# Attention loops of a two-layer model: the rows of scores are placed behind the products with the values

## The reference

```
xn = layernorm(x, g_in)
q = (xn @ Wq).reshape(b, n, 16, 64).transpose(0, 2, 1, 3) * scale
k, v = split(xn @ Wkv)                 # one head for all, after the null key and value
sim = einsum('bhid,bjd->bhij', q, k) + bias
sim = where(causal_mask, neg, sim); sim = where(mask_p, sim, neg)
attn = softmax(sim, axis=-1)
out = einsum('bhij,bjd->bhid', attn, v)
return layernorm(out.reshape(b, n, 1024) @ Wo, g_out)
```

## Time and profile before

| | us |
|---|---|
| median of 3 runs | 3386.32 (3378.21 to 3391.15) |
| the profiled execution | 3392.3 |
| its span, first to last instruction | 3390.5 |
| TensorE busy | 3055.6 (90%) |
| VectorE busy | 1947.1 (57%) |
| ScalarE busy | 1551.8 (46%) |
| GpSimd busy | 289.9 (9%) |

### The profile page before, as it was taken

The page is one execution under the profiler, slowest core; times in us unless marked ns, Lnnn a source line. Parts: engine busy times, 40 slices in busy tenths (PEclk is TensorE's granted clock), DMA queues, the critical chain, the costliest instruction groups (busy, mean ns, idle before and its releaser), DMA issues. The chain is left out here.

```text
span 3390.5 us, 50330 instructions
## 1 busy us (share of the span) xinstructions
PE 3055.6 (90%) x17338; PEld 2117.3 (62%) x17338; DVE 1947.1 (57%) x4655; ACT 1551.8 (46%) x3708; POOL 289.9 (9%) x605
## 2 busy tenths in 40 slices
PE   7999799989999999855879999997999999959996
PEld 5555566654677777533457777775477777736764
DVE  3556455535676765785757777535477677442223
ACT  1110355542666664454446666524266666313332
POOL 0003000000011110000000000000011111002222
PEclk8998899989999999886989999998999999979998
DMA  1007433127344441010542222102734444341112
GB/s 39 19 14 161 52 47 47 14 74 222 114 140 130 145 134 46 1 29 2 156 121 80 70 82 69 41 2 74 222 117 148 120 144 136 117 145 34 33 34 90
DMA packets 233450, 293.70 MB, mean 87 GB/s; under 512 B 25502, under 2 KB 178334, under 8 KB 233073
## 3 DMA queue, kind: packets, MB, share of 16 engines
q1 hardware_dynamic: 229466, 280.39, 29.8%
q0 software_dynamic: 3744, 10.23, 1.0%
HBM read 222.01 MB, written 68.10 MB: 86 GB/s over the span
## 5 line engine op out<-in xcount | busy, mean ns | idle before, releaser
L2076 ACT ACTIVATE cond_p<-cond_p,cond_negm 128x128 f32<-128x128 f32 (+7 forms) x768 | 593.1, 775 | 419.9 <-DVE cond_negm L2107 419.2
L2057 PE MATMUL ps_o<-cond_pt,cond_v 128*64 128x256 f32 (+1 forms) x3840 | 480.5, 371 | 5.2 <-DVE attn_out L2143 0.5
L2035 PE MATMUL ps_s<-cond_k_high,cond_q_high 128*128 128x512 f32 (+3 forms) x1152 | 443.5, 391 | 15.9 <-DVE cond_negm L2107 7.7
L2107 DVE CUSTOM_DVE_ANT_0 cond_p<-ps_s,cond_side,cond_null_scores 128x128 f32<-128x128 f32 (+7 forms) x512 | 404.0, 811 | 32.2 <-PE ps_s L2037 26.1
L2037 PE MATMUL ps_s<-cond_k_both,cond_q_both 128*128 128x512 f32 (+3 forms) x1152 | 390.4, 351 | 0.0
L2047 PE MATMUL ps_t<-ident,cond_p 128*128 128x128 f32 x2304 | 350.5, 282 | 6.7 <-ACT cond_pt L2081 4.8
L2057 PEld LDWEIGHTS ps_o<-cond_pt,cond_v 128*64 128x64 f32 x3840 | 237.9, 136 | 168.5 <-issue 70.7
L2047 PEld LDWEIGHTS ps_t<-ident,cond_p 128*128 128x128 f32 x2304 | 251.0, 141 | 107.2 <-issue 78.4
L1179 ACT ACTIVATE attn_pt<-ps_t 128x512 f32<-128x512 f32 (+3 forms) x384 | 172.7, 490 | 251.3 <-PE ps_t L1140 196.8
L2035 PEld LDWEIGHTS ps_s<-cond_k_high,cond_q_high 128*128 128x128 f32 x1152 | 222.7, 193 | 49.3 <-DVE cond_negm L2107 20.1
L2115 DVE COPY cond_pt<-ps_t 128x512 f32<-128x512 f32 (+1 forms) x240 | 140.3, 585 | 167.3 <-PE ps_t L2047 165.5
(11 more groups left out here) (430 smaller groups left out, 4782.9 us busy)
## 6 DMA issues: line engine op xcount, KB each, us to landing
mqa_q_halves<-cond_q_cut SPq DMA_DIRECT2D x96, 512.0 KB, 5.8
cond_q_both<-mqa_q_halves SPq DMA_DIRECT2D x384, 128.0 KB, 3.3
cond_q_high<-mqa_q_halves SPq DMA_DIRECT2D x192, 128.0 KB, 2.9
cond_side<-in_fside_16xSxS SPq DMA_DIRECT2D x32, 512.0 KB, 7.3
moe_experts<-in_L_ffn_W SPq DMA_DIRECT2D x16, 1024.0 KB, 12.3
cond_side<-in_fside_16xSxS SPq DMA_DIRECT2D x32, 448.0 KB, 5.8
cond_side<-in_fside_16xSxS SPq DMA_DIRECT2D x32, 384.0 KB, 5.1
cond_side<-in_fside_16xSxS SPq DMA_DIRECT2D x32, 320.0 KB, 4.6
```

The costliest lines, as they stand in the source:

```text
L2035: nc.tensor.matmul(m.S[k % 2][:, lo:hi], c32(a.Q1[i][:, h, s * P:(s + 1) * P]), c32(a.K1[:, keys]), start=True, stop=False)
L2057: last = nc.tensor.matmul(sums[u % ON][h * HD:(h + 1) * HD, s0 * P:2 * P], a.V[:, b * QB + kb, :], PT[c % PT_SLOTS][:, (2 * h + s0) * P:(h ...
L2076: nc.scalar.activation(p, p, ACT.Exp, bias=negm[u % SMALL][:, r:r + 1], scale=-1.0, accum_out=rsum[u % SMALL][:, r:r + 1]).then_inc(exped, 1)
L2107: nc.vector.tensor_tensor_reduce(out=probs(u, r, 0, q + 1), in0=m.S[k % 2][:, 0:L], in1=toep_back(u, h, L) if cosine else a.side[h][:, SID ...
```

## The change

The first of the two calls of `place` in each group is gone. It stood between the group's turns and its spread and attends, and placed up to two rows. The second call, behind the attends, now places all rows of the group. Nothing else differs: the same instructions, waits, buffers and transfers. (Lines from there on have a number lower by one.)

More of the change, by code:

```diff
@@ L1331, in mqa_order @@
                 finished = u
-            place(ROWS_AHEAD, 2)
             if spreads and n_groups - spreads[0][0] >= 2:
```

## The result

The changed kernel took **3506.68 us** (median of 4 runs, 3503.06 to 3515.6) against 3386.18 (4 runs, 3378.21 to 3391.15): a ratio of 1.0359, with a 95% interval of 1.0337 to 1.0382. It is slower by 120.5 us in the medians, and by 110.8 in the two profiled executions (3503.06 against 3392.3). The prediction was 3500, with 3420 to 3560 as its range.

What follows compares the result with a forecast made beforehand. TensorE was taken to bound the kernel, with VectorE and ScalarE hidden behind it. Pauses of 101 us, 8 for GpSimd waits and 6 for slow clock make 115; 3392 + 115 - 6, rounded, gives 3500 us, range 3420 to 3560.

Steps and rivals of the forecast that it cites:

- The round: One round of the loops, four units in ten groups: TensorE idles 2.2 us more, 101 us over 46 rounds.
- The chain: Sums on VectorE, exponential and turn copy on ScalarE lose attends as cover: TensorE idles 1.2 and 0.5 us a round.
- the first pause: Third group of a round: its first turn waits for ScalarE's copy, TensorE idle 1.2 us.
- the second pause: Fourth group of a round: its first turn waits for ScalarE's copy, 10.2 against 9.65, 0.5 us idle.
- The four small rows: Rows of 1, 2, 1, 2 blocks follow each other with two score buffers: TensorE idle 0.5 us a round.
- The switches of TensorE: TensorE's changes between kinds of work: cost taken as nothing; 0.1 us on some 460 groups would be 46 us.
- GpSimd and the half clock: Spreads wait 8 us more for GpSimd's copy; half clock speed behind two more long waits costs 6 us.
- The cover is enough: Rival, 15%: the chain fits its cover nearly everywhere, only the four small rows cost; 3423 us.
- The clock falls too: Rival, 8%: half speed on TensorE follows each round's pauses, adding 3 us a round, 138 in all; 3640 us.
- Faster: Rival, 5%: the chain fits its cover, biases transfer earlier, waits for GpSimd and some slow clock go; 3361 us.
- No difference: Rival, 4%: the gain and the four small rows' 23 us cancel; 3386 us.
- What would show it: Signs in the loops: TensorE busy 99.5% to some 93%, clock 1.00, turns waiting for ScalarE's copy about 90 times.

Runs made afterwards that it cites:

- E3: Changed kernel, with two of the four small rows (one and two blocks) placed ahead of the attends again: 3496.77 us, ratio 1.0326.
- e10: Changed kernel, with two of the four small rows ahead of the attends again and GpSimd's last mask one unit later: 3449.52 us, ratio 1.0197.
- e7: Kernel before the change, with GpSimd's mask of the last quarter of the biases one unit later in its queue: 3362.12 us, ratio 0.9936.
- e9: Changed kernel, with GpSimd's mask of the last quarter of the biases one unit later in its queue: 3467.18 us, ratio 1.0251.

## Why the prediction was right, and where it was not

**The round** was to grow by 2.2 us and grew by 2.24 in the second loop. The mechanism of two of its parts was right; that the sum came out so close was luck, with its parts off in both directions.

**The chain**: predicted pauses of 1.2 and 0.5 us, together 1.7 a round; measured 1.04 and 0.25 in the usual round (1.25 and 0.28 in the one that was followed), and 1.1 a round by the short exponentials. The place, the engines and the first pause were right. Two things were mis-sized. The first is the second pause. By my steps TensorE would reach that turn at 9.65 and the copy be seen at 10.2; it reached it at 10.03 (1939.93 less 1929.90) and the turn began at 10.31. TensorE was later than I had it by 0.4: 0.3 at the first pause, the rest in the switches. The chain was later by only 0.1, since ScalarE's spread copy begins 0.46 us after a turn's copy (1935.99 to 1936.45), not 0.57. A pause of TensorE is cover for the chain's next pass: pauses in one loop don't simply add. The second is the base. I wrote that between the starts of the earlier trace rows no time is lost, and 0.18 us a round was, at the attend of 1947.34, which waited for the late product. The change took this pause away, so the chain's net cost is 1.3 − 0.18 = 1.1.

**The four small rows**: predicted 0.5, measured 0.45 to 0.50 as a distance. E3's round is 0.41 shorter and e10 faster by 18 us, 0.38 in each of 46 rounds. Right.

**The switches of TensorE**, which I cost at nothing: this step failed. I took attend to row for turn to row and left out the third pair, turn to attend. Two full turns take 0.84 us ahead of a row, and 0.96 ahead of an attend (1929.90 to 1930.86); turns with a half one took 0.76 ahead of an attend and 0.63 ahead of a row. Some of it comes back where rows now stand ahead of turns: a row of seven takes 0.92 there and took 0.98 ahead of attends. What remains is 2.24 − 1.1 − 0.5 = 0.64 us a round, 30 us over 47 rounds. The bound that I named for this step, 46 us at 0.1 us a group, was of the right kind, and I should have taken something from it.

**GpSimd and the half clock**, predicted 8 + 6 = 14 us: the waits grew from 20.0 to 22.0 us, in 11 times and not 14, the clock behind them took about 3 us less and not 6 more, and e7 and e9 together give 1.4 us in the profiled executions. As a size it was too large there; the timed runs allow up to the full 14, and beyond. This stays open.

In all, over 47 rounds: chain 1.1 × 47 = 52 (predicted 78), small rows 0.5 × 47 = 24 (23), switches 0.64 × 47 = 30 (0). With 1.4 for GpSimd and the clock this makes 107, against 110.8 in the profiled executions; with the 15 that the medians give, 121 against 120.5. Two errors of some 25 to 30 us, one each way, cancelled.

**The rivals.** *The cover is enough* is refuted: turns waited 46.0 us in 55 times. *The clock falls too* is refuted: with pauses in every round the granted clock is 1.00 from 1780 to 2180. The swing that the Trainium skill, TensorE: Matmul & The Clock Gate, section "A second HAM failure mode: psum-queue depth-cycling", reports for short pauses does not show here at pauses of up to 1.25 us, twice in some 30 us. *Faster* needed a chain 1 us shorter, and the last mask shows that its 25 us are real but come from another edit (a gain of the early product there is, the 0.18 us a round at the attend). *No difference* fell with it.

**What would show it.** The busy share was to fall to 93%, and it fell to 96.2%. The time lost is as said (7% fewer instructions in the stretch), but the modelled ends cover part of it, and I had myself called distances the safer reading. For the same reason the waits are listed 55 times and not 90: the second pause of each round is in none of the lists. Durations stayed, the product waited longer for the spread's copy, and all of the extra time lies in the loops, as said.

## What to carry to other kernels

Where one engine is full and the others hide behind it, ask what lies between an instruction that starts a chain and the instruction that needs its end: the products between a row of scores and the next transposes were the time in which sums, exponential and copy ran. Moving work that no one waits for cost 3.6% here with no instruction added. Undoing one link of such a chain moved the wait in these runs (the late product to the attends, the small rows to the long row's buffer, the long rows to the seams of two orders), so judge an edit by the length of a round, not by the wait that it removes. And check on several rounds that the one you read instruction by instruction is the usual one.

## What the hardware showed beside it

- Two turns on TensorE ahead of an attend are 0.12 us longer than ahead of a row (0.96 against 0.84), with the same instructions and no wait listed. It is so with short exponentials too (0.97 in the new order, 0.85 in the old one). The trace doesn't tell why.
- Waits of TensorE cost more than their length in the first and third loops: 20.0 us of waits for GpSimd in the old order cost 29.9 us, and 22.0 in the new one 31.3. The clock behind some of them explains most of it: an estimated 8 of the 9.9 us beyond the waits in the old order, 5 of the 9.3 in the new one. It did not go by the length of the wait alone: it was 0.72 in the 6 us behind one of 1.83 us (907.13) and 1.00 behind one of 3.19 (2718.43). The rest stays open. Pauses of 1.04 to 1.25 us, one in nearly every round, left the clock at 1.00 in the second loop.
- A modelled end can hide a pause of 0.28 us fully, and of 1.25 us in part (1.06 listed).
